# Top-2 expert loop: the up weights of a tile copied four tiles ahead, with a semaphore of their own

## What is computed

```python
weights, indices = jax.lax.top_k(gate_logits, TOP_K)      # TOP_K = 2
weights = jax.nn.softmax(weights, axis=-1)
combine = jnp.zeros((N, E)).at[jnp.arange(N)[:, None], indices].add(weights)
for e in range(E):                                        # E = 8
    h = jax.nn.silu(xf @ w1[e].T) * (xf @ w3[e].T)        # 128 -> 384
    y = h @ w2[e].T                                       # 384 -> 128
    out = out + combine[:, e:e + 1] * y
```

## Time and profile before

| | |
|---|---|
| median of 3 runs | 778.28 us (776.01 to 778.66) |
| the profiled execution | 781.1 us, its span 779.3 us |
| share of the span, by the page | PE 68%, DVE 50%, ACT 45%, POOL 45% |
| expert loop, first scatter to last scatter | 542.6 to 753.6 us of the span |
| behind it | the results read back, weighted, added and written, to the end of the span |

### The profile page before, as it was taken

The page is one execution under the profiler, slowest core; times in us unless marked ns, Lnnn a source line. Parts: engine busy times, 40 slices in busy tenths (PEclk is TensorE's granted clock), DMA queues, the critical chain, the costliest instruction groups (busy, mean ns, idle before and its releaser), DMA issues.

```text
span 779.3 us, 12795 instructions
## 1 busy us (share of the span) xinstructions
PE 526.4 (68%) x4449; PEld 419.5 (54%) x4449; DVE 389.9 (50%) x1030; ACT 346.9 (45%) x731; POOL 350.3 (45%) x343
## 2 busy tenths in 40 slices
PE   4999732215394755059999989756787878878750
PEld 2445531211153634037777768745787877867750
DVE  5365657788520112398999998582111111111117
ACT  1112135534331121037777773305665756666645
POOL 2000000000268887347888873005666666667630
PEclk9999855556787687558999995556998989999985
DMA  9701146000045463720000002343111111111129
GB/s 302 317 27 28 40 86 162 0 0 0 17 125 116 95 143 35 177 49 2 3 3 3 3 2 69 82 101 106 45 45 41 42 42 45 41 42 48 39 70 284
DMA packets 65245, 56.05 MB, mean 72 GB/s; under 512 B 10176, under 2 KB 59200, under 8 KB 65056
## 3 DMA queue, kind: packets, MB, share of 16 engines
q1 hardware_dynamic: 49904, 38.46, 17.3%
q0 software_dynamic: 10688, 14.04, 8.2%
q10 hardware_dynamic: 4592, 2.75, 1.3%
HBM read 35.38 MB, written 19.86 MB: 71 GB/s over the span
## 4 chain that ended last, share of the span: by engine, by line
PE 37%; POOL 16%; DVE 15%; issue 14%; ACT 9%; DMA 5%; another core or an unknown queue 3%; ACTq 1%; POOLq 0%; DVEq 0%; SPq 0%
PE psum L1605 8%; PE psum L1342 7%; POOL arena L553 6%; PE psum L1611 6%; PE psum L1621 5%; PE psum L1321 4%; ACT arena_b L1272 2%; POOL scratch L499 2%; ACT arena_b L1157 2%; POOL v_x L543 2%; POOL y_even L509 2%; POOL x_tok L536 2%; POOL x_tok L560 2%; ACT arena_b L1155 1%
## 5 line engine op out<-in xcount | busy, mean ns | idle before, releaser
L1082 DVE TENSOR_TENSOR arena<-arena,psum 128x384 f32<-128x384 f32 x71 | 39.3, 554 | 182.6 <-PE psum L1611 86.3
L499 POOL DMA_INDIRECT scratch<-table,idx x32 | 33.7, 1054 | 210.6 <-DVE idx_w L839 201.1
L576 POOL DMA_INDIRECT arena<-normed,gather_i x71 | 73.8, 1040 | 63.7 <-DVE gather_i L1058 41.9
L584 POOL DMA_INDIRECT results<-arena,dest_i x71 | 72.9, 1026 | 58.8 <-ACT arena L1294 45.4
L1605 PE MATMUL psum<-arena,arena_b 128*128 128x128 f32 x426 | 72.6, 312 | 38.7 <-ACT arena_b L1272 25.3
L1605 PEld LDWEIGHTS psum<-arena,arena_b 128*128 128x128 f32 x426 | 60.0, 213 | 45.7 <-ACT arena_b L1272 29.2
L553 POOL TENSOR_TENSOR arena<-arena,peak 128x1024 f32<-128x1024 f32 x32 | 60.9, 1903 | 30.2 <-DVE peak L927 30.2
L1272 ACT COPY arena_b<-w_sb 128x768 f32 x71 | 58.7, 826 | 23.9 <-issue 23.9
L1342 PE MATMUL psum<-scratch,conv_sb 128*128 128x512 f32 x144 | 65.0, 606 | 0.0
L1611 PE MATMUL psum<-arena,arena_b 128*128 128x128 f32 x426 | 65.0, 293 | 0.0
L1321 PE MATMUL psum<-cst,arena 128*128 128x128 f32 x327 | 58.4, 295 | 8.1 <-DMA arena<-normed,gather_i 6.9
(11 more groups left out here) (249 smaller groups left out, 1125.4 us busy)
## 6 DMA issues: line engine op xcount, KB each, us to landing
arena<-in_w_down_dram SPq DMA_DIRECT2D x8, 768.0 KB
w_sb<-in_w_dram SPq DMA_DIRECT2D x3, 1536.0 KB, 12.8
x_tok<-in_x_dram SPq DMA_DIRECT2D x4, 512.0 KB, 8.0
y_odd<-zeros SPq DMA_DIRECT2D x4, 512.0 KB
table<-xn SPq DMA_DIRECT2D x8, 256.0 KB, 2.3
y_even<-x_tok SPq DMA_DIRECT2D x16, 128.0 KB
extra<-y_odd ACTq DMA_DIRECT2D x4, 512.0 KB, 11.7
x_tok<-y_even SPq DMA_DIRECT2D x4, 512.0 KB, 10.6
```

The costliest lines, as they stand in the source:

```text
L499: nc.gpsimd.indirect_dma_start(out=rows_b[:, e // 4 % 4, e % 4, :], out_offset=None, in_=table[:, :], in_offset=bass.IndirectOffsetOnAxis( ...
L576: nc.gpsimd.indirect_dma_start(out=rows_d[:, t % ROWS_D, :], out_offset=None, in_=normed[:, :], in_offset=bass.IndirectOffsetOnAxis(ap=gat ...
L584: nc.gpsimd.indirect_dma_start(out=results[:, :], out_offset=bass.IndirectOffsetOnAxis(ap=dest_i[:, t:t + 1], axis=0), in_=yx_d[:, t % OUT ...
L1082: nc.vector.tensor_tensor(act_d[:, b, :], silu_d[:, b, :], psum[:, 4 + b, 0:FF_D], ALU.mult).then_inc(e_act, 1)
```

## The change

The down weights get a semaphore of their own, `e_w2`. The up weights of tile t + 4, instead of t + 3, are copied in iteration t, behind silu(t + 2). Those of tile 3 go between the first two silus. The down weights stay where they were. Numbers of buffers, copies and waits of the copies themselves are the same.

```diff
@@ down_weights
                 nc.scalar.copy(w2_t[:, t % 4], w2_sb[:, bass.ds(e, 1), :, :]
-                               .rearrange("p e k h -> p (e k) h")).then_inc(e_w, 1)
+                               .rearrange("p e k h -> p (e k) h")).then_inc(e_w2, 1)
@@ ScalarE's loop
-            for t in range(2):
-                silu(t)
+            silu(0)
+            tile_weights(3)
+            silu(1)
             for t in range(RUN_D):
                 if t + 2 < RUN_D:
                     silu(t + 2)
+                if t + 4 < RUN_D:
+                    tile_weights(t + 4)
                 if t + 3 < RUN_D:
-                    tile_weights(t + 3)
                     down_weights(t + 3)
                 evac_y(t)
@@ up
-                pe.wait_ge(e_w, 2 * t + 1)
+                pe.wait_ge(e_w, t + 1)
@@ down
-                pe.wait_ge(e_w, 2 * t + 2)
+                pe.wait_ge(e_w2, t + 1)
```

More of the change, by code:

```diff
@@ L389, in metaformer @@
         f_scaled = sem("f_scaled")
-        e_tr, e_xt, e_h1, e_h3, e_silu, e_act, e_yp, e_y, e_w, d_wout = (
-            sem(f"e_{s}") for s in ("tr", "xt", "h1", "h3", "silu", "act", "yp", "y", "w", "wout"))
+        e_tr, e_xt, e_h1, e_h3, e_silu, e_act, e_yp, e_y, e_w, e_w2, d_wout = (
+            sem(f"e_{s}") for s in ("tr", "xt", "h1", "h3", "silu", "act", "yp", "y", "w", "w2", "wout"))
         e_ld = [sem(f"e_ld{i}") for i in range(ROWS_D)]
```

## The result

The change gives 775.0 us (median of 20 runs) against 778.5 us of the kernel before on the same chip: a ratio of 0.995, 95% interval 0.9931 to 0.9968. The kernel is faster, by 3.5 us, where 26 were predicted; 752 us and the range of 746 to 768 were both missed. (The text ahead has a wrong size in two places: the blocks work on 4096 tokens, and it is 8192 pairs that are sorted into the 71 tiles. No number of the prediction rests on it.)

A forecast was written before the change was run, and what follows sets the result against it. GpSimd was taken as the bound: 178.2 us of work in a 211.0 us loop, 32.8 waiting, nearly all for evac_y. Less about 2 and 5, 26 us were won: 778.28 to 752 us, range 746 to 768.

The forecast's parts named there:

- The wait of up for the copy goes away: Before up on TensorE: idle time put down to the copy falls from 25 us to under 5.
- What up waits for then is evac_y(t - 4): At up(t): evac_y(t - 4) becomes the last thing awaited, giving up 1.1 us in which ACT may be late.
- The ring at 2.24 us against 2.12: Up, silu, copy, next up: 2.24 us a tile at full clock against TensorE's 2.12, costing little if ACT is on time.
- The late starts of ACT are still there, in number and size: ScalarE instructions reading PSUM start late, in some 17 bunches in the loop; the change leaves these as they were.
- the bound of 164 to 187 us for ScalarE's loop: ScalarE's 127 us of own work plus 37.0 to 60 us of late starts; it keeps up with GpSimd's 178.
- The size of the gain: GpSimd's 32.8 us of waiting in the loop, less about 2 for the last scatters and 5 for bunches: 26 us.
- The late starts stay on the path to POOL: Rival, chance 0.22: late evac_y still holds its scatter, about 15 waits of 1.5 us stay; gain 9 to 14, 764 to 769.
- The sign of a miss: In the changed profile: GpSimd's waits for evac_y above 20 us would mean late starts pass to it directly.
- The follow-through of the bunch at 583 to 592 us: up(18) starts near 584.2, not 587.69; GpSimd waits 1.78 us once, not twice, and TensorE's clock stays.
- The clock: Loop's granted clock rises from 0.92 to nearly 1.00; rival, chance 0.06: short waits bring half clock, above 783 us.
- The rules: Skill rules weighed: short idle times can swing the clock; improving the busiest engine first names TensorE, gain near nothing.
- The rival "Nothing changes": Chance 0.08: lateness grows to fill the time, ScalarE bounds the loop at its present 211 us; 776 to 780 us.

The follow-up runs named there:

- plain_before: Kernel before the change, with rows from the seventh tile on brought by plain transfers in token order instead of GpSimd's gathers; 724.5 us, ratio 0.9295.
- plain_rows: Changed kernel with rows of tiles 6 to 70 loaded by plain SP-queue DMAs in token order instead of GpSimd's gathers; 717.4 us, ratio 0.9203.
- dve_w2: Changed kernel with the copy of the down weights moved from ScalarE to VectorE; 779.5 us, ratio 0.9979 to the kernel before.
- two_gathers: Changed kernel scattering only the last six tiles, with every tile gathered twice, the second time into an unread tile; 776.2 us, ratio 0.9946.
- fill_after: Changed kernel with four more unread 128x128 products on TensorE behind each tile's down group; 785.6 us, ratio 1.0095.
- no_gather: Changed kernel without the gathers of tiles 6 to 70, the first six tiles' rows being used again; 713.4 us, ratio 0.9147.
- pool_busy: Changed kernel with plain row transfers in token order and two GpSimd fills of an unread tile replacing each gather; 751.1 us, ratio 0.9643.

## Why the prediction was wrong

- **The wait of up for the copy goes away.** Right, and wholly: none of the 27 waits that are left is for the copy.
- **What up waits for then is evac_y(t - 4).** Right, and it is where the gain was lost: up starts 0.10 behind it (evac_y ends at 567.21, up starts at 567.31), evac_y is itself late, and 38.6 us of idle time before up became 38.2.
- **The ring at 2.24 us against 2.12.** Right in size where nothing disturbs it: 0.11 us a tile (plain_before, plain_rows), 7 us of the kernel if TensorE sets the pace. In this kernel GpSimd sets it, and the ring is of use only inside bunches.
- **"The late starts of ACT are still there, in number and size."** This is the step that failed, and with it the bound of 164 to 187 us for ScalarE's loop. I had added them to ScalarE's work as a fixed amount. They are not work of ScalarE: with 36 us less to do it waits more (dve_w2), and in the changed kernel those over 0.7 us grew from 58.8 to 68.4 us though the loop got shorter. They are TensorE's signals coming late. ScalarE's waits in the loop stayed at 78 us in all (78.7 and 77.6) and with its 127 us of work fill it. The reading that led there was wrong too: I had said that evac_y at 583.62 started 1.31 us after everything that it waits for was there. 1.31 is ScalarE's idle time; its semaphore was raised at 583.60, and that of the silu at 586.42 at 586.40. "Remote" said that the view could not name the releaser, not that there was none.
- **The size of the gain.** I expected 26 of GpSimd's 32.8 us of waiting to go, with only three or four bunches leaving a wait. The loop still has 206.3 - 178.2 = 28.1 of it. 16 waits of GpSimd for evac_y are of 1.37 to 1.94 us, one in nearly every bunch, and beyond the ordinary 0.31 they are 22.8 us. That is the rival "The late starts stay on the path to POOL", with a chance of 0.22, whose sum has 15 such waits and 22 us. Its 764 to 769 us missed too: the other 5.3 us are shorter waits, most of them between the last scatters, for which I had put 2, and the medians are 3.5 us apart where these two loops are 4.7.
- **The sign of a miss.** I had written that if GpSimd's waits for evac_y stay above 20 us, the late starts pass to it directly. They are 34.1 us, and were 45.4 with 4.8 ahead of the first scatter: 40.6 to 34.1. The other sign, late starts of over 75 us, depends on what is counted: 68.4 over 0.7 us, 77.6 with the short ones, and that sum was 78.7 before.
- **The follow-through of the bunch at 583 to 592 us.** Right for the single bunch: at 566 to 572 us GpSimd waits once (1.94) and not twice. Wrong for their sequence: I took the time won at one bunch as won for good, but the next bunch comes four tiles later whatever the program does with it.
- **The clock.** The rival that feared it was wrong: 0.93 in the loop against 0.92. So was my hope for nearly 1.00. two_gathers and fill_after have the late starts at 1.00.
- **The rules.** The busy shares would have named TensorE, whose tile at 2.12 us is indeed the pace once the hold-ups are gone (2.08 in no_gather). The 0.3 us in front of each DMA of GpSimd do count: where it waits for nobody, a gather and a scatter take 2.68 us, though it is recorded busy for 1.04 + 1.03 = 2.07 of them. The changed kernel's share of 45% on the page doesn't show how near GpSimd is to being the bound.
- **The rival "Nothing changes"** had a chance of 0.08 and comes nearest: 775.0 lies in the 774 to 783 that I gave it. Its reason, "lateness that grows to fill the time", fits ScalarE's rows, though it is TensorE's lateness; its own number, 776 to 780, missed the 3.5 us.

What the runs show of the cause: late starts appear in the kernel before and in all eleven others in which GpSimd starts two indirect transfers a tile, at best one every 1.3 us, and in none of the five with one a tile, whether TensorE or GpSimd is the bound. It makes no difference whether they are gathers, scatters or both, whether TensorE waits for the gathered rows, or whether TensorE idles beside them. What they block is open. 31 MATMUL stand behind the group that is waited for, and then the signals over 26 MATMUL come in 0.32 us, where TensorE takes 0.11 for one when it works in time. From 545 to 740 us, 59 of the changed kernel's 178 distances between one recorded signal of a product group and the next are under 0.2 us, against 2 of 199 in no_gather. So these are ends, or their signals, that are held back and come together, and not multiplications that take longer. That a product is ready in PSUM while its signal is held is argued and not shown, and so is any reason for the hold-up. A rate between one in 1.3 us and one in 2.1 wasn't tried, so where they begin isn't known either.

The Trainium skill ("SBUF — State Buffer", Who interferes with whom) says that a DMA never contends with a compute engine. For plain transfers the runs agree: plain_rows moves as many bytes without a late signal. If it is meant to cover indirect transfers of GpSimd at this rate, they disagree: TensorE, ScalarE and VectorE have the same instructions in no_gather as in the changed kernel, and ScalarE's waits of 2 us are in one and not in the other. The measurement decides; whether the transfer or GpSimd's preparing of it is in the way, and on what path, no run here tells.

## What to carry to other kernels

Before counting idle time of an engine as its own work, find whose result it waits for and match instruction to instruction from an undisturbed place: a TensorE that is recorded as busy may be far from having delivered. Stops of TensorE in the middle of a group (0.16 to 0.36 us here), within 0.04 us of a late reader's start, were the sign in this trace. If indirect transfers of GpSimd follow each other without a pause beside a chain of small matmuls, take half of them away in a trial: here the kernel became 8.5% shorter (no_gather), 3.6% with GpSimd kept about as busy (pool_busy), while reordering what waits on the hold-ups was worth 0.5%. Neither is a gain that can be had: both leave out the real rows.

## What was not expected

- Two indirect transfers a tile, 1.3 us apart, cost the kernel 24 us against a GpSimd that is about as busy with one transfer and two fills (775.0 and 751.1 us; loops of 206.3 and 180.1).
- ScalarE waits 3.30 us for TensorE while TensorE is recorded as busy for 4.00 of 4.00 us (fill_after). In the changed kernel the longest waits of ScalarE and VectorE are 3.4 and 7.0 us.
- Signals of TensorE come up to 7.1 us after the recorded end of their product group, and 0.01 us after it where GpSimd starts one indirect transfer a tile.
- With rows by plain transfers of the same size, TensorE runs 71 tiles in 145.8 us at a granted clock of 1.00, with none of this.
